# Layer 0's turned norm behind layer 1's logits on TensorE

## The reference

```
h = _layernorm(x, axis=-1) * (1 + c) + s
x = x + g * part(h)
```

```
q = (x @ w_q).reshape(b, n, HEADS, DIM_HEAD).transpose(0, 2, 1, 3)
k = (x @ w_k).reshape(b, n, HEADS, DIM_HEAD).transpose(0, 2, 1, 3)
gates = jax.nn.sigmoid((x @ w_gate).reshape(b, n, HEADS, EXPERTS).transpose(0, 2, 1, 3))
values = jnp.einsum('bhne,ehdk,bnd->bhnk', gm, value_experts, x)
```

## Time and profile before

| | us |
|---|---|
| median of 3 runs | 762.74 |
| lowest, highest | 762.21, 762.9 |
| the profiled execution | 763.29 |
| its span, first to last instruction | 761.5 |
| TensorE busy in it | 736.4 (97%) |
| VectorE busy | 550.3 (72%) |
| ScalarE busy | 382.0 (50%) |
| GpSimd busy | 189.6 (25%) |

### The profile page before, as it was taken

The page is one execution under the profiler, slowest core; times in us unless marked ns, Lnnn a source line. Parts: engine busy times, 40 slices in busy tenths (PEclk is TensorE's granted clock), DMA queues, the critical chain, the costliest instruction groups (busy, mean ns, idle before and its releaser), DMA issues.

```text
span 761.5 us, 16813 instructions
## 1 busy us (share of the span) xinstructions
PE 736.4 (97%) x6551; PEld 555.6 (73%) x6551; DVE 550.3 (72%) x1642; ACT 382.0 (50%) x1063; POOL 189.6 (25%) x235
## 2 busy tenths in 40 slices
PE   7899999999999999999999999999999899999996
PEld 5566757775786578657865776578578778999996
DVE  4877785868766876787678767877968754255997
ACT  3755656355535554565456545652562436554422
POOL 0232521154015401540154015303310422000000
PEclk9999999999999999999999999999999999999999
DMA  7950020402040204020402030203203404000000
GB/s 233 380 130 1 29 57 2 111 2 57 10 104 1 57 11 102 2 56 14 101 1 56 20 95 2 56 23 91 57 2 94 130 2 112 1 1 1 15 22 22
DMA packets 56342, 43.07 MB, mean 57 GB/s; under 512 B 38540, under 2 KB 49444, under 8 KB 54856
## 3 DMA queue, kind: packets, MB, share of 16 engines
q1 hardware_dynamic: 56264, 42.01, 20.6%
HBM read 32.42 MB, written 9.58 MB: 55 GB/s over the span
## 4 chain that ended last, share of the span: by engine, by line
PE 82%; DVE 11%; POOL 2%; ACT 2%; issue 1%; DMA 1%; SPq 0%; DVEq 0%; ACTq 0%
PE ps L1764 15%; PE ps L1844 14%; PE ps L1904 8%; PE ps L2069 4%; PE ps L2047 4%; PE ps L1750 4%; PE ps L2016 4%; PE ps L1772 4%; PE ps L1798 3%; PE ps L1785 3%; DVE shared L1491 2%; DVE shared L1484 2%; PE ps L1712 2%; PE ps L1927 2%; PE ps L1939 2%; PE ps L1685 2%
## 5 line engine op out<-in xcount | busy, mean ns | idle before, releaser
L1764 PE MATMUL ps<-veF,hB 128*128 128x512 f32 x256 | 121.3, 606 | 0.0
L1310 DVE COPY_PREDICATED shared<-ghot,ps 128x512 f32<-128x512 int32 x128 | 88.0, 726 | 3.3 <-PE ps L1764 0.5
L856 ACT ACTIVATE sc<-sc,nmax 128x128 f32<-128x128 f32 (+1 forms) x128 | 57.2, 448 | 58.7 <-DVE nmax L1296 58.7
L1764 PEld LDWEIGHTS ps<-veF,hB 128*128 128x128 f32 x256 | 45.2, 189 | 51.2 <-issue 40.2
L656 POOL TENSOR_TENSOR sc<-sc,rg 128x384 f32<-128x384 f32 x64 | 51.7, 829 | 69.5 <-DVE rg L1283 69.5
L713 POOL TENSOR_TENSOR ve<-mv,eps 128x2 f32<-128x2 f32 x24 | 8.6, 359 | 237.5 <-DVE mv L1196 237.5
L1844 PE MATMUL ps<-early_masks,oeF 128*128 128x256 f32 x256 | 62.9, 385 | 0.5 <-issue 0.5
L1844 PE MATMUL ps<-wide,oeF 128*128 128x256 f32 x256 | 62.3, 386 | 0.0
L2047 PE MATMUL ps<-hE,veF 128*128 128x256 f32 x256 | 59.5, 382 | 0.4 <-ACT wide L966 0.4
L1904 PE MATMUL ps<-hC,early 128*64 128x128 f32 x1024 | 59.2, 274 | 0.3
L1904 PEld LDWEIGHTS ps<-hC,early 128*64 128x64 f32 x1024 | 55.8, 137 | 2.8 <-issue 1.8
(11 more groups left out here) (253 smaller groups left out, 1521.8 us busy)
## 6 DMA issues: line engine op xcount, KB each, us to landing
chosen<-hot_scratch SPq DMA_DIRECT2D x16, 512.0 KB, 5.8
v_scratch<-shared SPq DMA_DIRECT2D x16, 512.0 KB, 5.3
vg<-v_scratch SPq DMA_DIRECT2D x16, 512.0 KB, 5.3
veF<-in_L_ffn_value_experts SPq DMA_DIRECT2D x1, 2048.0 KB, 10.0
oeF<-in_L_ffn_output_experts SPq DMA_DIRECT2D x1, 2048.0 KB, 14.6
early<-in_L_attn_w_qkv SPq DMA_DIRECT2D x1, 1536.0 KB, 15.5
shared<-bias_scratch SPq DMA_DIRECT2D x2, 512.0 KB, 6.3
veF<-in_L_ffn_W SPq DMA_DIRECT2D x1, 1024.0 KB, 5.2
```

Of the source, the lines that this page charges most:

```text
L856: act.activation(v, v, ACT.Exp, bias=nmax[:, h % RING, t:t + 1], scale=-1.0, accum_out=denB[:, h * T + t:h * T + t + 1]).then_inc(s_("f_e" ...
L1310: dve.copy_predicated(val[:, t, :].rearrange("p (h k) -> p h k", h=HF), ghot[:, t * HF:(t + 1) * HF, e].bitcast(I32).unsqueeze(2) .broadca ...
L1764: pe.matmul(ps[:, vbank(j), :], tok(hB, t), veF[:, :].rearrange("p (h e k) -> p e h k", h=HF, e=EF)[:, e, :, :], start=True, stop=True).th ...
```

## The change

In the six rounds the small step MODULATE of `after_attn0` for batch b + 2 no longer stands at the place "s" of `front1`, ahead of the logits, but at the beginning of `products`, behind the logits and ahead of the step QKV.

```diff
-            in_front = {"qk7": (ADD,), "v": (NORM,), "s": (MODULATE,)}
+            in_front = {"qk7": (ADD,), "v": (NORM,)}
+            in_products_first = {"start": (MODULATE,)}
...
                 front1(b, k + 1, beside((after_attn0, b + 2, k + 1, in_front), *more))
-                more = [] if last else [(attn0, b + 3, 0, in_products0)]
+                more = [(after_attn0, b + 2, k + 1, in_products_first)]
+                if not last:
+                    more.append((attn0, b + 3, 0, in_products0))
                 if not first:
                     more.append((after_attn1, b - 1, k + 2, in_products))
                 products(b + 1, beside((after_front1, b, 0, softmax), *more))
```

## The result

| | before, us | after, us |
|---|---|---|
| median of 4 runs each | 762.82 | 755.74 |
| lowest, highest | 762.21, 763.54 | 754.58, 756.62 |
| profiled execution | 763.29 | 754.58 |
| its span | 761.5 | 752.8 |

The ratio of after to before is 0.9906, with a 95% interval of 0.9888 to 0.9924: 7.1 us less, where 5.8 were forecast. The interval reaches from 5.8 to 8.5 us. The profiled pair differs by 8.7 us, because before's profile is of a run near its slowest and after's of its fastest; so totals are taken from the runs, and the profiles serve to see where the time went.

The account below looks back on a forecast made before the run. TensorE, busy 97%, was taken as the bound, with only its rests to win. Six rounds at 0.96 us give 5.8 us: 763.29 becomes 757.5 profiled, the median 762.74 becomes 756.9; range 755.7 to 758.6.

Parts of the forecast that it names:

- The rest that goes: TensorE's six waits, 4.1 us in all, before layer 1's two transposes for VectorE's normalized tile; claimed covered by the logits moved forward.
- The sum of a round: Query projection starts at 209.60 in place of 210.56, 0.96 us less; over six rounds 5.8 us, between 3.2 and 6.7.
- the choice of 0.39 between 0.22 and 0.52: Price in us of the two transposes behind the logits: 0.39 taken from a pair behind ordinary matmuls, bounded by 0.22 and 0.52.
- The floor of the query projection: It waits for the value evacuations, so cannot start before 209.45; TensorE arrives at 209.60, a margin of 0.15 us.
- The first rival: Query projection finds the evacuations unfinished every round; gain only 0.7 us a round, 4.2 in all: 758.5 us; chance 12%.
- VectorE behind the stretch: VectorE gains 0.35 us of TensorE's 0.96; the missing 0.6 comes from its later rests of 0.88 and 1.24 us.
- The second rival: VectorE's later steps set the pace; a round gains only 0.35 us, 2.1 in all: 760.6 us; chance 5%.
- Nothing else in the stretch keeps its own time: Around the changed stretch: loads come at the start, transfers of values and masks are used a stage later; no further term.
- the slower rival: New sequencer gaps of 0.45 us appear behind the changed stretch; three a round lose 2.3 us: 765.1 us; chance 3%.
- the range's low end: Total time: 762.74 less 6.7, less 0.3 for the spread of the runs, gives 755.7 us.
- What the gap is: TensorE's 0.45 us rest before the first product at 213.87, counted as "issue"; the prediction said no run shows its cause.

## Why the prediction was wrong, and which of its steps held

*The rest that goes, right.* All six waits for the tile are gone, and nothing came in their place. The sum of a round said 0.96 us, from 207.18 + 2.03 + 0.39; it measured 0.99 (6.82 less 5.83). On the chain, where the prices were read, values, logits and transposes took 3.44, 2.02 and 0.37 us where 3.44, 2.03 and 0.39 were forecast. So the choice of 0.39 between 0.22 and 0.52 came out, and a tile that is a microsecond early does not by itself bring the pair to 0.22. On the timeline the same 5.83 us divide into 3.53, 2.02 and 0.28, as a group's first start there is not where the chain ends the piece before.

*The floor of the query projection, right.* The evacuations end 0.15 us before the projection is due, about the margin that was forecast, and no wait shows. The first rival didn't come about, and no experiment priced it.

*VectorE behind the stretch, right.* Its rests of 0.35 and 0.88 us were taken up, 1.02 of 1.24 are left, and the later stretches of the rounds keep their length. The second rival fell.

*"Nothing else in the stretch keeps its own time", wrong: this is the step that failed.* It put everything behind the stretch at nothing, and spoke of the data alone, which is used a stage later. The exchange that starts behind the evacuations does keep its own time, and the transfers of TensorE's instructions are counted on the same engines. With the rest for the tile gone, round 1's block comes ahead of the exchange: its first instruction starts 5.01 us behind the transfer in place of 1.36. With that a stall of 0.65 us in round 1 and 0.1 to 0.4 in round 4 went. I had the stall in the rows, 0.45 us ahead of the first product, and gave it to the slower rival, with the sign reversed: I asked whether closing the rest could bring more of such stalls, and not what ended this one. That is the missing microsecond: 5.9 (6 x 0.99) + 0.65 + 0.1 to 0.4 + 0.2 is 6.9 to 7.2, against 5.8 in the forecast. By the ratio, before's 762.74 becomes 755.6, just below the range's low end of 755.7; that end took in the spread of the prices, and no gain from a stall. That the runs' totals alone hold more than the six stretches is not shown: the intervals hold 6.0 us too, and stalls and the fallen clock of 0.4 to 1.2 us come and go. The gain beyond 6.0 us is shown by the stretches.

*What the gap is.* The prediction could not tell; the transfers show that it is a block of instructions that came late.

What stays open is when a block is asked for, and why the one near 348 us comes late without an exchange beside it.

## What to carry to other kernels

Where one engine is busy for 97%, look at each of its rests for the one instruction that waits, and put ready work of the same queue in front of it; the gain is the rest (here 0.68 us) and what the waiting pair cost above a ready one (0.52 less 0.28), times the rounds. Then look at the pauses without a cause too: compare two profiles of the same kernel, and a pause that stands at the same place in both has a reason that a change nearby can remove or make worse. Where the trace has the instruction transfers, look when the block that begins at the pause came in. Take totals from the runs and places from stretches between fixed points of the program, since single profiles differed by 1 to 2 us here.

## What the runs showed of the hardware

TensorE paused for up to 1.53 us in the rounds with all its data at hand. Each such pause stood where a block of 256 of its instructions begins, and ended 1.3 to 1.6 us behind the end of that block's transfer. In round 1 the block was late because its transfer started 1.7 to 2.9 us behind the first of a large exchange (share of the transfer engines 0.69 and 0.83); the pause vanished with the exchange cut, with the exchange 1.7 us later, and with the block's transfer ahead of the exchange (from 204.22 where the exchange began at 206.84). Near 348 us a block was late with a share of 0.00 to 0.06.

The Trainium skill (Runtime: NRT & Kernel Launch, Instruction fetch mechanics) has instructions refilled in blocks of 16 KiB. The 0.85 MB in 52 packets on the page of before agree with it. The same section of the Trainium skill has that refill hidden behind the issue of instructions. These traces show refills that were not hidden, with the times above, and there the measurement decides.
